# Cross attention and an MXINT8 feed-forward layer: weight units interleaved over two slots, their quotients on GpSimd

## The reference

```
q = ctx Wq^T + bq ; k = ctx Wk^T + bk ; p = softmax(q k^T)        # ctx 512 x 256, p 512 x 512
x = x + layernorm(x) p^T
h = layernorm(bf16(layernorm(x))) * ln_w + ln_b                   # 512 x 512
y = gelu(mx(h) mx(W1)^T + b1)                                     # W1 2048 x 512
x = x + bf16(v + mx(y) mx(W2)^T + b2), v = bf16(layernorm(x))     # W2 512 x 2048
mx(a): per block of 32: scale = 2^floor(log2 amax) / 64 ; clip(round(a / scale), -128, 127) * scale
```

## Time and profile before

| what | value |
|---|---|
| median of 3 runs | 283.56 us (282.99 to 286.78) |
| the profiled execution | 283.25 us, of which the traced span is 281.4 us |
| busy, share of the span | PE 81%, VectorE 89%, ScalarE 60%, GpSimd 25% |
| chain that ended last | VectorE 45%, PE 25%, ScalarE 11%, DMA 8%, issue 5%, GpSimd 4% |
| mean granted clock of PE | 0.927 |

### The profile page before, as it was taken

How to read it: one execution, slowest core, us unless ns; L and a number is a source line. 1 busy time by engine, 2 the same in 40 slices (tenths; PEclk the granted TensorE clock), 3 DMA queues, 4 the chain that set the end, 5 groups by cost and what they waited for, 6 DMA issues and landing times.

```text
span 281.4 us, 3244 instructions
## 1 busy us (share of the span) xinstructions
PE 228.7 (81%) x937; PEld 99.4 (35%) x946; DVE 249.2 (89%) x377; ACT 169.4 (60%) x287; POOL 69.0 (25%) x96
## 2 busy tenths in 40 slices
PE   7748739996998059651699969799999989999993
PEld 7314313443433024210244433344444434444431
DVE  2388999999988899999979999599999999877992
ACT  2337216628995447845987599966566554665610
POOL 1058100022004500053060050413333233333400
PEclk9985886999999759975899999999999999999999
DMA  4963999999997952939623045635355555555683
GB/s 157 378 250 89 227 279 201 297 238 194 263 257 190 221 91 38 222 59 194 124 52 62 0 93 70 119 62 123 88 122 129 130 130 131 130 130 114 139 178 130
DMA packets 103077, 42.92 MB, mean 152 GB/s; under 512 B 93844, under 2 KB 96152, under 8 KB 102552
## 3 DMA queue, kind: packets, MB, share of 16 engines
q1 hardware_dynamic: 100224, 35.93, 58.6%
q10 hardware_dynamic: 2360, 6.83, 7.7%
q0 software_dynamic: 480, 0.02, 0.1%
HBM read 15.48 MB, written 4.19 MB: 70 GB/s over the span
## 4 chain that ended last, share of the span: by engine, by line
DVE 45%; PE 25%; ACT 11%; DMA 8%; issue 5%; POOL 4%; SPq 2%; ACTq 0%; DVEq 0%; POOLq 0%
DVE amax L764 12%; PE ps L722 9%; PE ps L712 8%; PE ps L661 4%; DVE w_int L807 4%; DMA xhl<-pf 3%; DVE hq L966 3%; DVE stats L918 3%; DMA wst<-in_L_ffn_W 3%; DVE vw L961 3%; DVE pf L871 3%; DVE phl L942 2%; DVE wquant L861 2%; POOL rs L350 2%; DVE xhl L954 2%
## 5 line engine op out<-in xcount | busy, mean ns | idle before, releaser
L661 PE MATMUL ps<-pT,xT 128*128 128x512 f16 x192 | 49.7, 414 | 14.1 <-DMA pT<-phl 11.0
L722 PE MATMUL ps<-w2T,xhl 128*128 128x512 bf16 x247 | 56.5, 379 | 2.9 <-DMA xhl<-pf 2.4
L712 PE MATMUL ps<-w1T,cxT 128*128 128x512 bf16 x256 | 58.0, 380 | 0.0
L558 ACT ACTIVATE wst<-ps 128x1024 bf16<-128x1024 f32 x32 | 32.3, 1019 | 27.9 <-PE ps L712 27.9
L764 DVE TENSOR_REDUCE amax<-phl 128x64 f32<-128x2048 bf16 x16 | 36.5, 2280 | 6.9 <-ACT phl L562 6.9
L649 PE MATMUL ps<-qkT 128*128 128x512 f32 x32 | 19.5, 715 | 22.7 <-ACT pf L457 18.8
L661 PEld LDWEIGHTS ps<-pT,xT 128*128 128x128 f16 x192 | 19.9, 106 | 48.0 <-issue 31.8
L722 PEld LDWEIGHTS ps<-w2T,xhl 128*128 128x128 bf16 x256 | 24.6, 98 | 33.2 <-DMA xhl<-pf 4.2
L712 PEld LDWEIGHTS ps<-w1T,cxT 128*128 128x128 bf16 x256 | 23.7, 98 | 32.6 <-issue 6.2
L562 ACT ACTIVATE phl<-wst 128x2048 bf16<-128x2048 bf16 x16 | 30.6, 1910 | 1.3
L423 POOL TENSOR_TENSOR wst<-wst,vs 128x512 bf16<-128x512 bf16 x12 | 14.8, 1233 | 55.5 <-DVE wquant L866 55.5
(11 more groups left out here) (79 smaller groups left out, 357.4 us busy)
## 6 DMA issues: line engine op xcount, KB each, us to landing
wst<-in_L_ffn_W ACTq DMA_DIRECT2D x6, 1024.0 KB, 6.1
xs<-in_x SPq DMA_DIRECT2D x4, 1024.0 KB, 8.4
out_x<-wst SPq DMA_DIRECT2D x16, 256.0 KB, 2.8
cx<-in_ctx SPq DMA_DIRECT2D x4, 512.0 KB, 5.8
wst<-in_L_ffn_W SPq DMA_DIRECT2D x2, 1024.0 KB, 10.3
xhl<-pf SPq DMA_TRANSPOSE x17, 4.3
xT<-xhl SPq DMA_TRANSPOSE x16, 4.6
pT<-phl SPq DMA_TRANSPOSE x16, 3.3
```

Of the source, the lines that this page charges most:

```text
L558: act.activation(ys[:, k, 1024 * g:1024 * g + 1024], ps_y[:, 2 * g:2 * g + 2, :], ACT.Copy)\
L661: pe.matmul(ps_pv[:, t % 2, :], xT[:, t, NT * a + n, :], pT[:, :, NT * c + n, :], start=(s == 0), stop=False)
L712: last = pe.matmul(ps_y[:, c, :], h1T[:, k, t, :], w1T[:, 4 * c:4 * c + 4, t, :], start=False, stop=(t == KT - 1))
L722: last = pe.matmul(ps_z[:, k, :], h2T[:, k, t, :], w2T[:, t, :], start=False, stop=(t == FT - 1))
```

## The change

The two slots no longer stand for W1 and W2. The even slot takes three units of W1 and one of W2, the odd one a unit of W1 and three of W2, so that all of W1 is quantised a batch sooner. The quotients of the odd slot's four units are made by GpSimd, in place and as f32 (`over_scale`), at the head of the next batch; VectorE clips them straight from `wst` (`w_clip_product`). The first two tiles' `product1` stand ahead of the values of batch 3, ScalarE evicts them apart from their GELU, and the normalising of batch 2 moves behind the first GELU tiles, into the slots of VectorE. In ScalarE's batches `v_sums` and `v_out` stand one tile later, and the odd load behind step 6.

```
+        UNITS = (("w1", 0), ("w1", 2), ("w1", 3), ("w2", 2)), (("w1", 1), ("w2", 0), ("w2", 1), ("w2", 3))
 SyncE, front(b)
                 for t in range(NT):
+                    if b == B - 1 and t == NT - 1:
+                        sp.wait_ge(h1_step, H_STEPS)
+                        sp.wait_ge(qk_ps, 2 * B)
+                        h1_transpose(0, 0)
+                        h1_transpose(0, 1)
 GpSimd
+            def over_scale(u):
+                pool.wait_ge(w_step[ODD], W_STEPS * u + 4)
+                w = blocks(wst[:, ODD, :])
+                inverse = mxi[:, ODD, :, 0:1].broadcast_to([P, NB, BLOCK])
+                pool.tensor_tensor(w, w, inverse, ALU.mult).then_inc(w_step[ODD], 1)
+            pool.wait_ge(w_step[EVEN], W_STEPS)
+            over_scale(0)
+            factors_x(2)
+            mean_x1(0)
+            pool.wait_ge(w_step[EVEN], 2 * W_STEPS)
+            over_scale(1)
+            factors_x1(0)
+            factors_x(3)
+            factors_v(0)
+            mean_x1(1)
+            pool.wait_ge(h_rdy, LT)
+            over_scale(2)
+            factors_x1(1)
+            factors_v(1)
+            mean_x1(2)
+            factors_x1(2)
+            pool.wait_ge(h_rdy, 2 * LT)
+            over_scale(3)
+            factors_v(2)
 ScalarE, after the batches
             for t in range(LT):
                 v_out(B - 2, t)
+            act.wait_ge(w_step[EVEN], W_STEPS * (B - 1) + 5)
+            y_evict(0, 0)
             v_sums(B - 2, 0)
             v_sums(B - 2, 1)
+            y_evict(0, 1)
             v_sums(B - 2, 2)
             v_sums(B - 2, 3)
             for t in range(NT):
                 act.wait_ge(pT_rdy[t], 16 * B)
-            for k in range(2):
-                x_plus(B - 1, k)
-                y_out(0, k)
-            x_plus(B - 1, 2)
-            x_plus(B - 1, 3)
-            for t in range(LT):
-                x1_square(B - 1, t)
+            gelu(0, 0)
+            x_plus(B - 1, 0)
+            gelu(0, 1)
+            for t in range(1, LT):
+                x_plus(B - 1, t)
+            x1_square(B - 1, 0)
+            x1_square(B - 1, 1)
             y_out(1, 0)
+            x1_square(B - 1, 2)
+            x1_square(B - 1, 3)
+            y_out(1, 1)
 PE
-            values(B - 1, 0)
-            pe.wait_ge(w1T_rdy, 16 * B)
+            pe.wait_ge(evenT_rdy, 16 * 3)
+            pe.wait_ge(oddT_rdy, 16)
+            product1(0, 0)
+            product1(0, 1)
             pe.wait_ge(p_exp, T)
-            for k in range(2):
-                if k > 0:
-                    values(B - 1, k)
-                product1(0, k)
-            values(B - 1, 2)
-            values(B - 1, 3)
+            for t in range(LT):
+                values(B - 1, t)
             product1(1, 0)
 VectorE, front(b)
                 negmax(b, 0)
+                if w1 is not None:
+                    w_amax(EVEN, w1)
+                negmax(b, 1)
                 normalise(b, 0)
-                if w1 is not None:
-                    w_amax(W1, w1)
-                negmax(b, 1)
                 normalise(b, 1)
+                if w2 is not None:
+                    w_clip_product(w2)
 ...
-                if w2 is not None:
-                    w_over(W2, w2)
 VectorE, back(b): w_clip and w_mult of the even slot now stand ahead of times_w and plus_b
 VectorE, after the batches
-            parts = tail_parts(B - 2)
-            for part in parts[:LT]:
-                for part_step in part:
-                    part_step()
-            slot(0, 0, parts[LT], True)
-            slot(0, 1, parts[LT + 1])
-            slot(1, 0, [])
+            p2, p3 = tail_parts(B - 2), tail_parts(B - 1)
+            slot(0, 0, [], True)
+            slot(0, 1, p2[0] + p2[1])
+            slot(1, 0, p2[2] + p2[3])
+            slot(1, 1, p2[LT])
+            slot(2, 0, p2[LT + 1])
+            slot(2, 1, p3[0])
+            slot(3, 0, p3[1] + p3[2])
+            slot(3, 1, p3[3] + p3[LT])
+            slot(4, 0, p3[LT + 1])
```

More of the change, by code:

```diff
@@ L210, in wait_alone, with load_unit @@
                 eng.sem_inc(gate, 1)
+        def load_unit(eng, slot, u):
+            kind, n = UNITS[slot][u]
+            if kind == "w1":
+                return eng.dma_start(wst[:, slot, :].rearrange("p (r k) -> p r k", r=4), w1_t[n])
+            return eng.dma_start(wst[:, slot, :], w2_t[n])
         @block.sync
@@ L266, in _ @@
             front(1, 3, 3)
-            with sp.Fori(2, B) as b:
-                front(b)
+            front(2)
             def h1_transpose(m, k):
@@ L511, in batch @@
             def batch(b, front, qk, v):
-                for t in range(LT + 1):
+                for t in range(LT + 2):
                     if t < NT:
@@ L518, in batch @@
                         x_high(front, t)
-                    if t > 0:
+                    if 0 < t <= NT:
                         p_high(front, t - 1)
-                    if b is not None and t > 1:
+                    if b is not None and 1 < t < LT + 1:
                         x_plus(b, t - 2)
-                    if t == 2 and b is not None:
-                        load_w2(front)
-                    if v is not None and t > 0:
-                        v_sums(v, t - 1)
-                    if v is not None and t < LT:
-                        v_out(v, t)
+                    if t == 1 and b is not None:
+                        load_odd(front)
+                    if v is not None and t > 1:
+                        v_sums(v, t - 2)
+                    if v is not None and 0 < t <= LT:
+                        v_out(v, t - 1)
                     if qk is not None and t == 2:
                         context(qk)
-                if not isinstance(front, int) or front + 1 < B:
-                    load_w1(front + 1)
+                    if t == LT and front + 1 < B:
+                        load_even(front + 1)
                 if b is not None:
@@ L571, in z_out, with step @@
                 act.activation(zs[:, k, :], ps_z[:, k, :], ACT.Copy).then_inc(z_sb, 1)
+            def step(m, k):
+                if not isinstance(m, int) or 2 * m + k + 3 < T:
+                    y_out(*tile(m, k, 3))
+                z_out(m, k)
             for t in range(LT):
                 v_out(B - 2, t)
+            act.wait_ge(w_step[EVEN], W_STEPS * (B - 1) + 5)
+            y_evict(0, 0)
             v_sums(B - 2, 0)
             v_sums(B - 2, 1)
+            y_evict(0, 1)
             v_sums(B - 2, 2)
@@ L581, in _ @@
                 act.wait_ge(pT_rdy[t], 16 * B)
-            for k in range(2):
-                x_plus(B - 1, k)
-                y_out(0, k)
-            x_plus(B - 1, 2)
-            x_plus(B - 1, 3)
-            for t in range(LT):
-                x1_square(B - 1, t)
+            gelu(0, 0)
[5 more added lines that the diff above has]
+            x1_square(B - 1, 1)
             y_out(1, 0)
+            x1_square(B - 1, 2)
+            x1_square(B - 1, 3)
+            y_out(1, 1)
             for t in range(LT):
                 v_out(B - 1, t)
-            def step(m, k):
-                if not isinstance(m, int) or 2 * m + k + 3 < T:
-                    y_out(*tile(m, k, 3))
-                z_out(m, k)
-            step(0, 0)
-            for t in range(LT):
-                v_sums(B - 1, t)
-            step(0, 1)
-            with act.Fori(1, T // 2 - 2) as m:
+            z_out(0, 0)
+            y_out(2, 0)
+            v_sums(B - 1, 0)
+            z_out(0, 1)
+            v_sums(B - 1, 1)
+            y_out(2, 1)
+            v_sums(B - 1, 2)
+            v_sums(B - 1, 3)
+            z_out(1, 0)
+            step(1, 1)
+            with act.Fori(2, T // 2 - 2) as m:
                 for k in range(2):
```

136 lines of the change are left out of this document (61 added, 75 removed).

## The result

The changed kernel takes 288.87 us (median of 4 runs, 287.2 to 291.94) against 283.34 us for the kernel before on the same chip: a ratio of 1.018 (95% interval 1.013 to 1.023). So it is 1 to 2% slower, inside the range of the prediction (278.5 to 290.5), 3.9 to 4.6 us above its forecast of 284.3.

A forecast was written before the change was run, and what follows sets the result against it. PE and VectorE were both taken as full in the feed-forward stage. Tile 9 0.7 us later made the span 281.4 + 0.7 = 282.1; with 1.85 above span and 0.3 to the median, 284.3 us, range 278.5 to 290.5.

The forecast's parts named there:

- the pricing of the odd load: ScalarE's queue in batch 2: the load's issue takes 0.4 us; even-slot loads move by under 1 us.
- Batch 1 and the lock: Batch 1's saved quotient is lost waiting for energies at 49.55; VectorE two-input or two-port operations and GpSimd operations exclude each other.
- The wait at the head: At a batch's head, `normalise` waits for GpSimd's product until 4.2 us, behind 3.4 us of maxima: 0.8 us a batch given back.
- Batch 2: ScalarE reaches tile 2's `p_high` 15.6 us after the head, so the saving is lost; 17.1 us more to batch 3 at 97.7.
- The stage change: Between batch 3 and feed-forward: PE idles nearly 4 us, low clock costs 1.6, first GELU ends 149.3, third tile at 164.1.
- rival (c): PE stays at the low clock through the second early product and batch 3's values: up to 4 us more, 288; chance 0.11.
- To tile 9: VectorE from third tile to tile 9: 52.1 us as before plus 7.5 for batch 2's normalising and quantising, reaching 223.7.
- (a): Rival: the saving comes through, VectorE is never late and PE alone decides: 278 us; chance 0.17.
- (b): Rival: GpSimd's product is long, at 5.8 us costing 5 us more, at 7 us giving 293; mark over 5.5; chance 0.12.

The follow-up runs named there:

- the later load: The changed kernel with ScalarE issuing the odd load one tile later, at its old place (t == 2 for t == 1): 285.28 us, ratio 1.001 to the kernel before.
- 32 KB: The changed kernel with its early odd load, but batch 1's load brings 32 KB instead of 1 MB, the rest left out: 285.95 us, ratio 1.012.
- the last two kernels: Later load, both new orders and `x_plus` ahead of `v_sums`: 280.91 us; the same with batch 2's normalising between tiles 1 and 2: 280.58 us.

## Why the prediction held, and the step that failed

The time lies in the range, and the path of the forecast is found again row by row. But the range is 12 us wide, and the slower side came about through something that the prediction did not price: that the range held is in part luck. "Again" is the second profile of the changed kernel; the right column is the kernel with the later load, in which the collision is absent.

| step | forecast | changed kernel | again | later load |
|---|---|---|---|---|
| GpSimd's product | 4.0 | 3.64 | 3.64 | 3.64 |
| head of batch 1 | 49.55 | 49.41 | 50.18 | 49.52 |
| batch 3 begins | 97.7 | 103.83 | 100.45 | 98.01 |
| last `v_sums` ends | 121.75 | 127.29 | 123.91 | 121.47 |
| `v_out` of batch 2 starts | 132.0 | 137.74 | 134.36 | 130.94 |
| second early product ends | 142.4 | 148.27 | 144.88 | 141.47 |
| first GELU ends | 149.3 | 155.28 | 151.90 | 148.49 |
| third tile at VectorE | 164.1 | 169.98 | 166.60 | 163.19 |
| tile 9 at VectorE | 223.7 | 231.13 | 227.74 | 224.33 |
| span | 282.1 | 290.1 | 286.7 | 283.3 |

**The step that failed** is the pricing of the odd load. The prediction said of the even slot's loads that they "move by under 1 us", and of the odd load only that its issue takes 0.4 us of ScalarE. That it leaves 5.4 us sooner, within 4 us of an x load and W1's transpose, was in the kernel and was not priced. From the head of batch 1 to that of batch 3 the forecast has 48.15 us (97.7 - 49.55). With the old place (one line) it is 48.49, with 32 KB 48.49; with the megabyte 54.42 and, in the second execution, 50.27. In medians the early load costs 2.9 us (288.16 to 285.28) of the 3.9 to 4.6 missed. The spans of the columns "again" and "later load" differ by 3.4 us: 1.8 of it are these batches, 1.0 is GpSimd's power, which the load does not explain, and 0.7 was there at the head of batch 1.

**Batch 1 and the lock.** The saving lost to energies is shown (2.04 us at 49.41). The wait at the head was sized at 0.8 us a batch, and is less: the pair of `normalise` takes 1.16 us in batch 3, where it takes 0.99 at 71.00, with no product beside it. So 0.2. With a product of 3.64 in place of 4.0 the forecast's own arithmetic would have given 0.4. That the two engines exclude each other is seen better behind the fourth product. VectorE:

```profile
140.00 1.41 DVE L808 TENSOR_SCALAR pow<-amax 128x64 uint32<-128x64 uint32 x1
```

and GpSimd, which ends at 141.37:

```profile
137.73 3.64 POOL L412 TENSOR_TENSOR wst<-wst,mxi 128x2048 f32<-128x2048 f32 x1
```

An operation of 0.17 to 0.2 us takes 1.41 and ends with the product, while the reduction at 137.68 ran on beside it in its usual 2.29 us. By the Trainium skill (SBUF — State Buffer, Who interferes with whom) a scalar operation of VectorE in a two-port mode and one of GpSimd shut each other out for a whole instruction, and a reduction is free of it. The trace agrees on both.

**Batch 2.** With the later load ScalarE sets the pace, as forecast: `p_low` of tile 2 comes 14.6 us behind the head, 15.7 forecast. From there to batch 3 it takes 18.15 us for 17.1, since the wait for GpSimd's factors is still 0.93 us (at 92.20) where none was forecast. The two misses of 1.1 us cancel, so that batch 3's head came out within 0.3 us is luck in part. The kernel with GpSimd's quotients alone shows the same bound, harder.

**The stage change.** Nearly exact. VectorE is idle for 7.76 us ahead of the first GELU (6 forecast), PE for 4.50 between its products (nearly 4), and the second product takes 5.31 us for 3.63 at the usual clock, 1.7 for the 1.6 forecast at a granted clock of 0.68. Of rival (c) nothing more was seen: the values behind it ran in 2.75. The last experiments confirm why the saving does not come through. Two queues in a fixed order each wait for the other, and only when both orders move, with `x_plus` ahead of `v_sums`, does 1.2% come free (ratio 1.001 to 0.990), some 3 us.

**To tile 9.** Mis-sized: 61.1 us from the third tile against 59.6. A part of it stands in VectorE's timeline of the kernel with the later load, where a first row of batch 3's normalising takes 1.64 us and not 0.75:

```profile
190.99 0.46 DVE L808 TENSOR_SCALAR pow<-amax 128x64 uint32<-128x64 uint32 x1
...
192.50 1.64 DVE L1002 SCALAR_TENSOR_TENSOR vw<-vs,mean,lnw 128x512 f32<-128x512 bf16 x1
```

while GpSimd's addition of x, 1.16 us long elsewhere, takes 2.12 beside it:

```profile
191.48 2.12 POOL L446 TENSOR_TENSOR wst<-xs,wst 128x512 f32<-128x512 f32 x1
```

Together with the power (0.46 where the neighbouring tiles have 0.35) that is 1.0 of the 1.5 us. GpSimd's additions come later in this tile than before, behind the small operations of batch 3's factors; that this order, new with the change, makes the two meet is read from the rows, and no run took it away.

**Rivals.** (a), the saving coming through at 278, needed another order on two engines; with it the last two kernels reach 281. How much of that is the saving is not shown: no run has the new orders with the quotients on VectorE. (b) is false by its mark: 3.64 us. The slower side came about through a mechanism that no rival named.

## What to carry over

When a step moves in a queue, price the transfers that it issues by what else is in flight at their new time, even if the move looks like a detail of the diff: here one megabyte 5.4 us sooner cost some 3 us, where the whole change was forecast at 0.7. Before work is taken off an engine, find the queue that it next waits for. Here 7 us less of VectorE left the kernel no faster than before (285.28 against 284.0) until PE's and ScalarE's orders at the stage change were altered together. And take the offset of the start out of two timelines before their later rows are compared.
